# Layer norms of batches 2 to 7 moved from before the first stage into it

## What is computed

```python
h  = layernorm(x) * (1 + ca) + sa            # norm "h", one per batch
xn = layernorm(h) * ln1_w + ln1_b            # norm "n", one per batch
q, k, v = xn @ q_w + q_b, xn @ k_w + k_b, xn @ v_w + v_b
attn = softmax(causal(q k^T / sqrt(8)))  @ v          # 16 heads of 8 channels
xz = xn @ in_proj_w                          # the state-space branch (mamba)
x_c = silu(conv4(xz[:256])); dt = softplus(x_c @ ... + dt_b)
state = exp(dt * A) * state + dt * x_c * B   # a scan over the 512 positions, 16 states
x1 = h + alpha * attn @ o_w + (1 - alpha) * ((y + x_c * D) * silu(z)) @ ssm_out_w
```

## Time and profile before

| | |
|---|---|
| time, median of 3 runs | 1876.72 us (1875.6 to 1885.94) |
| the profiled execution's own time | 1876.86 us |
| its span, first to last instruction | 1875.1 us |
| busy: PE, DVE, ACT, POOL | 1454.9, 1396.2, 1069.7, 848.3 us |
| mean granted TensorE clock | 0.891 of full speed |

### The profile page before, as it was taken

One profiled execution on the slowest core, in us unless ns is written; L12 is line 12 of the kernel. 1 busy time (PEld: TensorE's weight loads), 2 busy tenths in 40 slices (PEclk: granted clock), 3 DMA queues, 4 the chain that ended last, 5 costly groups with the idle time before them and its releaser, 6 DMA issues. The chain is left out here.

```text
span 1875.1 us, 21858 instructions
## 1 busy us (share of the span) xinstructions
PE 1454.9 (78%) x7058; PEld 911.6 (49%) x7090; DVE 1396.2 (74%) x2071; ACT 1069.7 (57%) x1784; POOL 848.3 (45%) x866
## 2 busy tenths in 40 slices
PE   4856667767677677776776678879999999986778
PEld 3333334334344343343333246458878787843673
DVE  2587977878878788788799258687867676858866
ACT  2745555555465455654555467567787878841107
POOL 3273646647565466565665431211222222236853
PEclk9966978989888898888899989989999999987889
DMA  3121202111121022111210020101111111100001
GB/s 80 55 81 52 67 27 66 57 50 58 49 68 61 25 66 66 51 54 43 66 63 18 1 89 18 49 15 51 46 40 46 39 50 42 45 6 1 1 1 45
DMA packets 61654, 84.72 MB, mean 45 GB/s; under 512 B 6588, under 2 KB 32038, under 8 KB 61542
## 3 DMA queue, kind: packets, MB, share of 16 engines
q1 hardware_dynamic: 61442, 83.30, 14.6%
q10 hardware_dynamic: 100, 0.03, 0.0%
HBM read 74.38 MB, written 8.78 MB: 44 GB/s over the span
## 5 line engine op out<-in xcount | busy, mean ns | idle before, releaser
L994 PE MATMUL bank<-QK 127*128 127x384 bf16 (+6 forms) x992 | 244.8, 330 | 173.3 <-DVE Mx L1243 148.1
L1686 POOL TENSOR_TENSOR dBx<-dtx,Bb 128x512 f32<-128x512 f32 x256 | 324.9, 1291 | 13.5 <-DMA Bb<-b_dram 8.8
L1296 DVE TENSOR_TENSOR hl<-lsq,hh 128x512 fp32r<-128x512 f32 x320 | 258.6, 819 | 78.2 <-ACT hh L1570 70.0
L1510 ACT ACTIVATE PT<-bank 128x512 f32<-128x512 f32 x320 | 186.8, 596 | 222.9 <-PE bank L994 150.9
L1263 DVE TENSOR_TENSOR_SCAN hst<-bank,dBx 128x512 f32<-128x512 f32 x256 | 298.0, 1204 | 4.8 <-POOL dBx L1686 4.8
L1567 ACT ACTIVATE lsq<-bank,vcol 128x512 f32<-128x512 f32 x320 | 218.9, 693 | 109.9 <-DVE hl L1296 73.5
L1243 DVE TENSOR_REDUCE Mx<-bank 128x1 f32<-128x384 f32 (+3 forms) x352 | 217.2, 629 | 83.5 <-PE bank L994 82.4
L1666 POOL TENSOR_SCALAR_AFFINE_SELECT PT<-PT 128x256 f32<-128x256 f32 (+1 forms) x320 | 116.4, 369 | 314.6 <-ACT PT L1510 314.4
L994 PEld LDWEIGHTS bank<-QK 127*128 127x128 bf16 (+1 forms) x1024 | 95.0, 108 | 329.6 <-DVE Mx L1243 213.8
L1705 POOL TENSOR_TENSOR stage<-stage,lrs 128x512 f32<-128x512 f32 x64 | 88.7, 1385 | 314.1 <-DVE lrs L1376 314.1
L994 PE MATMUL bank<-x,we1h 128*128 128x512 f32 x640 | 211.7, 413 | 24.5 <-DVE x L1284 14.7
(11 more groups left out here) (248 smaller groups left out, 2462.3 us busy)
## 6 DMA issues: line engine op xcount, KB each, us to landing
Bb<-b_dram SPq DMA_DIRECT2D x128, 256.0 KB, 3.6
stage<-w_rows SPq DMA_DIRECT2D x64, 256.0 KB, 3.3
parts<-part SPq DMA_DIRECT2D x16, 384.0 KB, 2.8
QK<-parts SPq DMA_DIRECT2D x64, 96.0 KB
QK<-parts SPq DMA_DIRECT2D x64, 64.0 KB
stage<-in_L_ffn_We_dram SPq DMA_DIRECT2D x16, 256.0 KB, 3.4
hst<-in_L_attn_x_dram SPq DMA_DIRECT2D x8, 256.0 KB, 5.8
QK<-parts SPq DMA_DIRECT2D x64, 32.0 KB
```

Source lines behind the costliest of these rows:

```text
L994: return engine.matmul(o, l, r, start=start, stop=stop, tile_position=pos, skip_group_check=True)
L1296: engine.tensor_tensor(hl[:, sl, :], full[:, f, :], hh[:, sl, :].bitcast(F32), ALU.subtract).then_inc(sems["dve_hl"], 1)
L1510: engine.activation(PT[:, it["sl"], :], o[:], ACT.Exp).then_inc(sems["act_exp"], 1)
L1686: engine.tensor_tensor(dBx[:, sl, h], dtx[:, b % 2, h], Bb[:, sl], ALU.mult).then_inc(sems["pool_dbx"], 1)
```

## The change

The 12 norms of batches 2 to 7 leave the front: only norm (1, "n") stays there, with the same 6 steps of the state-space branch. A new generator `norms_of(b)` does the two norms of one batch. It is advanced in the even units 0, 2, ... 10, for the batch two ahead (b = u/2 + 2), at a rate of 12 steps per 20 steps of `attend`, and it is run out at the unit's end. It takes bank c from the ring and removes that bank from it until the norm is finished; bank v is the one that the ring hands out next at the time of `ln_a`. The squares go to a `PT` tile in place of `lsq`, which the state-space branch uses as scratch. Between `ln_a` and `ln_b` of a norm lie four of its steps, that is 4 x 20/12 = 6.7 steps of `attend`. Line numbers of the changed kernel are 18 higher on the engines' programs.

```diff
--- before.py
+++ after.py
@@ -422,6 +422,19 @@
         if u % 2 == 1 and (u + 3) // 2 < NB:
             yield from project((u + 3) // 2)
 
+    def norms_of(b):
+        for r, kind, ready in ((r_h, "h", lnb[b]), (r_n, "n", None)):
+            k = take()
+            ring.remove(k)
+            sl = pts[0] % NPT
+            pts[0] += 1
+            f = p.norm_start((k, ring[0]), (ready or r_h[b],), kind=kind, b=b, square=f"PT{sl}", sl=sl)
+            for _ in range(4):
+                yield
+            r[b] = f()
+            ring.append(k)
+            yield
+
     banks = ((0, 4), (1, 5), (2, 4), (3, 5))
 
     def first_norms(order):
@@ -437,13 +450,13 @@
     mixer = mamba()
     drain(project(0))
     fetch(0)
-    run_together(p.norms(first_norms([(1, 1)] + [(b, l) for l in range(2) for b in range(2, NB)])), 12, (mixer, 6, False))
+    run_together(p.norms(first_norms([(1, 1)])), 1, (mixer, 6, False))
     fetch(1)
     run_together(maxima(0), 23, (chain(values_of(0), project(1)), 8, True), (mixer, OFF, False))
     tops = chain(*[maxima(u) for u in range(1, NU)])
     run_together(first(tops, LEAD), LEAD, (mixer, SSM_RATE * LEAD / 20, False))
     for u in range(NU):
-        run_together(attend(u), 20, (mixer, SSM_RATE, False), (tops, 23, False), (prepare(u), 8, True))
+        run_together(attend(u), 20, (mixer, SSM_RATE, False), (tops, 23, False), (prepare(u), 8, True), (norms_of(u // 2 + 2) if u % 2 == 0 and u // 2 + 2 < NB else iter(()), 12, True))
     while late or later:
         settle(0)
     drain(mixer)
@@ -984,6 +997,11 @@
                 return xT[:, b, :], n4[:, b // 2, :, b % 2, :], mod[:, 1, 1, b:b + 1], mod[:, 1, 0, b:b + 1]
             return xT[:, b, :], hT[:, b, :], mod[:, 1, 4, b:b + 1], mod[:, 1, 3, b:b + 1]
 
+        def square(it):
+            if "sl" in it:
+                return PT[:, it["sl"], :]
+            return win if it["kind"] == "ln4" else lsq[:, it["n"] % 2, :]
+
         def expert_bias(e, c):
             return col("ffn_b1", c) if e == 9 else col("bs1", c) if e == 8 else col("be1", 4 * e + c)
 
@@ -1018,7 +1036,7 @@
                     q.wait_ge(("pool_set", pool_set["cm"]), it["free0"], it["ready"], it.get("w4"))
                     mm(bank[it["banks"][0]][:], cmat[:], src).then_inc(sems["pe_lnc"], 1)
                 elif kind == "ln_b":
-                    sq = win if it["kind"] == "ln4" else lsq[:, it["n"] % 2, :]
+                    sq = square(it)
                     q.wait_ge(it["sq"], it["free1"])
                     mm(bank[it["banks"][1]][:], omat[:], sq).then_inc(sems["pe_lnv"], 1)
                 elif kind == "qk0":
```

## The result

The changed kernel takes 1933.62 us (median of 4 runs, 1931.47 to 1934.11), the kernel before 1880.10 in the same comparison: ratio 1.0266, 95% interval 1.0241 to 1.0290. The ratio isn't the quotient of the two medians. The kernel is slower by some 2.7%, where 1899 us and at most 1918 were forecast. The execution that the profile shows took 1931.47 us, with a span of 1929.7. The lines that the norms and waits bear have moved by 18: L994 is now L1012, L1181 is L1199, L1243 is L1261, L1494 and L1496 are L1512 and L1514, L1767 is L1785.

A forecast was written before the change was run, and what follows sets the result against it. Front: norms on TensorE, then the fetch's landing; stage: VectorE, busy for 87% of an even unit. 1876.86 us less 8 (front) plus 30 (six even units) gave 1899 us, range 1872 to 1918.

The forecast's parts named there:

- Slower had 0.70: Whole kernel: chance 0.70 that it becomes slower by over 0.5%, above 1886 us.
- the 52 to 55 us that were given as a sign: Stage: even units with norms would be 52 to 55 us long, unit 12 unchanged at about 48.
- The front: Before the stage: first maxima at 75.5 us after the landing, projection 9.3 us earlier, less 1.3 for the clock: 8 gained.
- 5 us. Six units: 30 us: Stage: two norms lengthen each even unit from 0 to 10 by 5 us, 30 us in all.
- the ring: Even units: two banks instead of three during norms make maxima wait; 2.7 us at most, 1.3 us counted per unit.
- the wait for the chain: Even units: VectorE stands some 1.5 us before each norm's multiplication, 3 us a unit, of which 2 counted.
- the 0.9 taken off for time that is idle anyway: Even units: 0.9 us subtracted from the 5.9 us sum because part falls where VectorE waits anyhow.
- VectorE's own work: Even units: the two norms add 2.1 us of VectorE instructions per unit.
- GpSimd's shift: Even units: norm "n" needs norm "h"'s shift from GpSimd; TensorE stands 3 us, 0.5 us counted per unit.
- rival 3: Stage: waiting for GpSimd's shift or the two-bank ring becomes the pace, 47 us in all, 1916 us; chance 0.15.
- The bounds: Stage cost from rows showing extra work: low 1.7 us a unit (10 in six), high 5.7 to 7.8 (34 to 47).
- rival 1: Stage: norms are hidden in even units' idle time, only the front counts; 1867 or 1869 us, chance 0.10.

The follow-up runs named there:

- short_hold: Changed kernel with one step in place of four between the two halves of a norm, so the bank is held shorter; 1904.71 us, ratio 1.0139.
- short_split: Changed kernel with one step between a norm's halves and its VectorE and GpSimd part one step later; 1885.07 us, ratio 1.0028.
- split: Changed kernel with the norm's last part on VectorE and GpSimd one norm step later, bank held that step longer; 1923.41 us, ratio 1.0242.
- ring_only: Kernel before, no norm moved, but one bank taken from the ring in the steps where norms would hold it; 1906.88 us, ratio 1.0149.
- odd_units: Changed kernel with the norms of batches 3 to 7 in odd units 1 to 9, batch 2 still in unit 0; 1955.09 us, ratio 1.0408.
- odd_short_split: Changed kernel with norms of batches 3 to 7 in odd units, one step between norm halves, VectorE's part one step later; 1871.45 us, ratio 0.9955.
- late_fetch: Changed kernel with the second unit's twelve transfers issued after unit 0's maxima instead of before; 1949.44 us, ratio 1.0373.

## Why the prediction was wrong, point by point

**Direction and place: right.** Slower had 0.70. The even units grow, though by more than the 52 to 55 us that were given as a sign, the odd ones and unit 12 nearly don't (+2.3 there, at a granted clock of 0.88), and VectorE's waits name `lrs`, as the text said they would.

**The front: right in sum, in part by luck.** I took 8 us, between 6 and 10; the stage starts 10.3 us earlier. The first maxima start at 78.73, not at 75.5: "the nearest transfers land 2.5 us (`parts`) and 3.8 us (`Bb`) after issue" gave a landing after 3.3 us, and it takes 6.1. The clock was at half speed as expected and cost about what was counted. Four multiplications of the maxima take 0.61 us now and 0.40 before, the values 1.92 and 1.13 (before, then changed):

```profile
86.79 1.13 PE L994 MATMUL bank<-wv,nT 128*128 128x128 f32 x8 [0.37 <-DVE Mx L1243]
```

```profile
81.05 1.92 PE L1012 MATMUL bank<-wv,nT 128*128 128x128 f32 x8
```

From the start of the maxima to that of the projection it makes some 2 us, my estimate from the starts of the same multiplications in the two kernels; the projection's first part then lasts 1.90 us in both. So the projection gained 4.95 us and not 9.3. The first scan gained 6.7 us.

Of the remaining 3.6 us up to the first Exp, 3.3 are not the norms' doing. They come from the projections of batch 1 to dt, B and C, whose 22 multiplications are the same in the kernel before, the changed one and short_hold (in this order):

```profile
159.18:166.33 7.15, 7.15 (x22) 4.03 (x23) 0.64 (x2) 2.33 (x4) 0.00 (x0) 0.50 0.17 50
```

```profile
152.53:156.34 3.81, 3.81 (x22) 2.29 (x23) 0.64 (x3) 2.33 (x4) 0.00 (x0) 1.00 0.04 9
```

```profile
152.66:159.80 7.14, 7.14 (x22) 4.02 (x23) 0.64 (x2) 2.32 (x4) 0.00 (x0) 0.50 0.17 42
```

Before, TensorE ran them at the half clock (1.2 GHz), after it had had nothing to do for some 3 us; in the changed kernel the granted clock stayed full (2.4 GHz) over a wait of the same length. Short_hold has the front of the changed kernel, instruction by instruction, and ran them at half clock; its stage starts at 172.3 us, only 6.5 earlier than before. That the sum of the front came out near 8 is therefore no proof of its terms: the landing was too early in it by 2.8 us, and the clock of a later place gave 3.3.

**The stage: the step that failed is "5 us. Six units: 30 us".** It is 10.3 a unit and 61.6 in six. The terms that failed are the ring, taken at 1.3 us a unit, the wait for the chain, taken at 2, and the 0.9 taken off for time that is idle anyway. The runs take this apart in the order of the edits:

| term, six even units (us) | forecast | measured | by |
|---|---|---|---|
| bank held over four steps | 1.3 x 6 = 7.8 | 28.6 | changed less short_hold |
| wait for the chain | 2 x 6 = 12 | 17.6 | short_hold less short_split |
| VectorE's own work | 2.1 x 6 = 12.6 | 15.4 | short_split less before |
| GpSimd's shift | 3 | none seen | no such wait of PE or DVE in unit 4 or 6 |
| time that is idle anyway | -5.4 | none | waits of VectorE grow by 7.9 us a unit |

The split between the first two rows depends on the order. With the later place first it costs 4.4 us (split), and the short hold then brings 50.6 (356.0 - 305.4); and the clocks of single units differ, as told at short_hold. What doesn't depend on an order is that the bank alone, with no norm behind it, costs 4.0 us a unit (ring_only), and that the two together bring 46.2 of the 61.6 us. So the term of the ring was mis-sized by a factor of three at least. It was worked out from the places where two maxima follow each other, "4 or 5 times 0.6", and half of that was taken. What it left out is that TensorE, while it stands for a bank, holds back everything behind it in its list, so that TensorE and VectorE, each in the order of its list, wait for each other in turn. A norm in unit 6 shows it, all engines in order of time:

```profile
582.89 0.68 DVE L1261 TENSOR_REDUCE Mx<-bank 128x1 f32<-128x512 f32 x1
...
583.72 1.17 PE L1012 MATMUL bank<-PT,omat 128*128 128x512 f32 x2 [1.81 <-DVE Mx L1261]
...
584.93 0.69 ACT L1512 ACTIVATE lrs<-bank,epsc 128x512 f32<-128x512 f32 x1 [3.08 <-PE bank L1012]
...
585.65 0.63 ACT L1514 ACTIVATE lrs<-lrs 128x512 f32<-128x512 f32 x1
...
586.31 0.75 DVE L1199 SCALAR_TENSOR_TENSOR hT<-bank,mod,lrs 128x512 f32<-128x512 f32 x1 [2.74 <-ACT lrs L1514]
...
587.16 1.56 POOL L1673 TENSOR_SCALAR hT<-hT,mod 128x512 f32<-128x512 f32 x1 [4.79 <-DVE hT L1199]
...
589.57 0.75 DVE L1199 SCALAR_TENSOR_TENSOR hT<-bank,avec,hT 128x512 f32<-128x512 f32 x1 [2.50 <-PE bank L1012]
...
589.64 1.07 PE L1012 MATMUL bank<-hT,cmat 128*128 128x512 f32 x2
```

The averaging (583.72) waits 1.81 us for VectorE to reduce the maximum of 582.89 and so free the bank that it writes. I had let that maximum run beside the chain and counted 1.5 us a norm; here VectorE ends the maximum, and then stands 2.74 us for averaging, Ln and Exp, nearly the whole free-running chain. In unit 4 the chain waits are 3.5 us for norm "h" and 1.7 for norm "n", 5.2 together and not 3, of which I counted 2. Next comes the output projection, whose four parts stand behind on TensorE: VectorE waits 2.50 us for it at 589.57. I had taken this wait, 1.24 us in the earlier trace rows, as cover; it grew instead. GpSimd's shift (587.16, 1.56 us long) is over before norm "n" comes to TensorE at 589.64, so rival 3 had one of its two reasons right, the two-bank ring, and the other wrong.

**The bounds failed too.** Both came from rows that say what more *work* costs: 1.7 us by the values, 7.8 by ScalarE's ratio. The lower one was misread besides: the row at 960.20 is no even unit without values but unit 13, an odd one whose projections are over, and VectorE has more work there (43.31 against 41.97 us), so the two rows don't differ by the values alone. And the 9.5 us in rival 1's 1867 stand nowhere else in the prediction; the projection's own 9.3 would have given the same. Ring_only adds no work and costs 4.0 us a unit, and odd_units has the same work as odd_short_split at 14.5 us more in each odd unit. In these kernels the price of two norms lies between nothing and 14.5 us a unit, by how long the bank is held and where the reader of the result stands. A ratio of work can't bound that.

**Rival 1** (hidden) is what happens in odd_short_split, in five units out of six: 12 norms in the stage for 3.5 us. Of the Trainium skill's advice on interleaving parts that load different engines ("Perfetto Trace Analysis", Optimization Strategy) this case's runs agree only there; as changed, the same interleaving cost 60 us in the pairs. Its remark on too few PSUM buffers behind a repeating gap agrees with ring_only: 4.0 to 7.9 us of waits for scores.

## What to carry to other kernels

Work that is spread into a full stage is priced by what it *holds* and where its last reader stands in the list of the engine that is the pace, before it is priced by its length. Take a bank out of a shared ring for as few steps as the data allow, and put the last part one step behind the point at which its chain can be done; only with both did the odd units of this kernel take the norms in. Before a move, look in the trace for who frees the bank that the moved step writes: if that is the engine which later waits for the step, as in unit 6 here, one wait stands behind the other.

## What the runs showed of the hardware that was not expected

First, the twelve transfers of a fetch land 6.1 us behind the last issue (78.73 and 78.15 us), and 158.86 - (144.82 + 7.77) = 6.3 us in the later fetch of late_fetch, against 2.5 and 3.8 us of the earlier trace rows, and the first fetch takes as long with twelve more behind it on the queue as with none. Second, the granted clock of the same 22 multiplications behind the same wait was 1.00 in the changed kernel and 0.50 in short_hold, which is worth 3.3 us of a start. It was also 1.00 in split and 0.50 in short_split, and each kernel has one profile, so whether the kernel or the execution decides it stays open. Third, in odd_short_split unit 5 has eight more multiplications than unit 5 of before, yet TensorE is busy for 50.91 us instead of 52.74: the granted clock of the stretch is 0.93 instead of 0.82. Whether a fuller list raised the clock, or the clock and the shorter waits have a common cause, these runs don't tell.
